# Self-attention band writes: issued by ScalarE on its own DMA queue instead of by the sync engine

## The reference: what is computed

```
scores = q @ k^T                                   # 512 x 512 per head
rel_q[l, r] = q[l] . dist_emb[l - r + 511]         # relative position, query side
rel_k[l, r] = k[r] . dist_emb[l - r + 511]         # relative position, key side
probs = softmax((scores + rel_q + rel_k) / sqrt(32))
ctx   = probs @ v
x1    = layernorm(x + layernorm(ctx @ Wo + bo + x) * gamma + beta)
```

## Time and profile before

| | |
|---|---|
| median of 3 executions | 4623.52 us (4620.94 to 4632.6) |
| profiled execution | 4626.37 us, span 4624.6 us |
| TensorE (PE) busy | 3912.8 us, 85% of the span |
| VectorE (DVE) busy | 2198.7 us, 48% |
| ScalarE (ACT) busy | 1738.2 us, 38% |
| GpSimd (POOL) busy | 1770.0 us, 38% |
| sync engine's DMA queue (q1) | 1158.57 MB, 68.4% of the 16 DMA engines' time |
| ScalarE's DMA queue (q10) | 7.34 MB, 0.4% |

### The profile page before, as it was taken

The page is one execution under the profiler, slowest core; times in us unless marked ns, Lnnn a source line. Parts: engine busy times, 40 slices in busy tenths (PEclk is TensorE's granted clock), DMA queues, the critical chain, the costliest instruction groups (busy, mean ns, idle before and its releaser), DMA issues. The chain is left out here.

```text
span 4624.6 us, 68626 instructions
## 1 busy us (share of the span) xinstructions
PE 3912.8 (85%) x19584; PEld 2380.7 (51%) x19584; DVE 2198.7 (48%) x6132; ACT 1738.2 (38%) x3691; POOL 1770.0 (38%) x1556
## 2 busy tenths in 40 slices
PE   6888888888888886769999999999899566788676
PEld 4666666666666664336666666666544342121144
DVE  4656565656565664854444444444433211111156
ACT  4656565656565663333333333333311110000023
POOL 3656565656565655324444444444411000000012
PEclk9999999999999998989999999999999788888898
DMA  6999898989898996454554445444365326999723
GB/s 265 377 346 363 337 363 335 367 335 373 332 376 331 373 355 252 158 188 155 164 166 153 156 164 167 155 154 164 113 179 166 124 88 274 409 410 411 305 76 134
DMA packets 566768, 1169.16 MB, mean 253 GB/s; under 512 B 35312, under 2 KB 225136, under 8 KB 517360
## 3 DMA queue, kind: packets, MB, share of 16 engines
q1 hardware_dynamic: 561968, 1158.57, 68.4%
q10 hardware_dynamic: 4032, 7.34, 0.4%
q0 software_dynamic: 512, 0.26, 0.0%
HBM read 762.63 MB, written 403.44 MB: 252 GB/s over the span
## 5 line engine op out<-in xcount | busy, mean ns | idle before, releaser
L437 POOL TENSOR_SCALAR a_sc<-a_sc,a_inv 128x512 f32<-128x512 f32 x512 | 809.3, 1582 | 603.4 <-DVE a_inv L387 540.7
L1002 POOL TENSOR_SCALAR b_sc<-b_sc,b_inv 128x128 f32<-128x128 f32 (+3 forms) x512 | 552.7, 1083 | 775.5 <-DVE b_inv L955 775.5
L273 ACT ACTIVATE a_sc<-a_sc,a_mx 128x512 f32<-128x512 f32 x512 | 370.1, 723 | 683.0 <-DVE a_mx L380 682.8
L914 ACT ACTIVATE b_sc<-b_sc,b_mx 128x128 f32<-128x128 f32 (+3 forms) x512 | 287.7, 562 | 815.2 <-DVE b_mx L949 815.1
L960 DVE COPY b_pt<-b_ps_t 128x128 f32<-128x128 f32 (+3 forms) x512 | 248.4, 485 | 575.5 <-PE b_ps_t L862 575.5
L380 DVE CUSTOM_DVE_ANT_0 a_sc<-a_ps_s,a_rq 128x512 f32<-128x512 f32 x512 | 353.3, 690 | 294.8 <-PE a_ps_s L175 263.9
L185 PE MATMUL a_ps_t<-a_ident,a_sc 128*128 128x128 f32 x2048 | 319.7, 279 | 118.6 <-DVE a_pt L394 113.2
L854 PE MATMUL b_ps_s<-b_kT,b_qz 128*128 128x128 f32 (+3 forms) x1024 | 361.0, 434 | 0.8 <-DVE b_mx L949 0.8
L173 PE MATMUL a_ps_s<-a_ks,a_qs 128*128 128x512 f32 x512 | 321.1, 627 | 47.4 <-issue 34.7
L283 ACT ACTIVATE a_stage_q<-a_ps_q 128x640 f32<-128x640 f32 x512 | 350.3, 684 | 18.0 <-PE a_ps_q L198 17.7
L283 ACT ACTIVATE a_stage_k<-a_ps_k 128x640 f32<-128x640 f32 x512 | 354.8, 693 | 1.7 <-DMA band_k<-a_stage_k 1.7
(11 more groups left out here) (202 smaller groups left out, 6264.2 us busy)
## 6 DMA issues: line engine op xcount, KB each, us to landing
band_q<-a_stage_q SPq DMA_DIRECT2D x128, 1280.0 KB, 6.3
band_k<-a_stage_k SPq DMA_DIRECT2D x128, 1280.0 KB, 9.1
a_rk<-band_k SPq DMA_DIRECT2D x128, 1024.0 KB, 11.4
a_rq<-band_q SPq DMA_DIRECT2D x256, 512.0 KB, 11.9
d_w<-in_e_W SPq DMA_DIRECT2D x32, 4096.0 KB, 38.7
b_xT<-x1T SPq DMA_DIRECT2D x64, 1024.0 KB, 5.7
b_cT<-in_ctxT SPq DMA_DIRECT2D x64, 1024.0 KB, 8.3
d_wg<-in_e_Wg SPq DMA_DIRECT2D x16, 4096.0 KB, 28.9
```

Of the source, the lines that this page charges most:

```text
L273: act.activation(sc[n][:, :], sc[n][:, :], ACT.Exp, bias=mx[:, n:n + 1], scale=-1.0, accum_out=sm[:, n:n + 1]).then_inc(sem["a_exped"], 1)
L437: pool.tensor_scalar(sc[n][:, :], sc[n][:, :], inv[:, n:n + 1], None, ALU.mult)\
L914: act.activation(sc[i][:, 0:width(i)], sc[i][:, 0:width(i)], ACT.Exp, bias=mx[:, i:i + 1], scale=-1.0, accum_out=sm[:, i:i + 1]).then_inc( ...
L1002: pool.tensor_scalar(sc[i][:, 0:width(i)], sc[i][:, 0:width(i)], inv[:, i:i + 1], None, ALU.mult).then_inc(sem["b_normed"], 1)
```

## The change

The function `write` and its call leave the sync engine's stream. ScalarE's stream gets a `write` of its own. It is called right behind `stage` when the staged tile was the last of its head, and issues the q and the k write, each behind a wait for the staging copies (its own engine's) and an increment of a new semaphore. Addresses, sizes and completion semaphores of the writes are the same, and so is all that waits for them.

```
# sync engine
-            def write(g, j, h):
-                for kind, st in (("q", stage_q), ("k", stage_k)):
-                    sp.wait_ge(sem[f"a_{kind}_staged"], NT * g + T4 * h + T4)
-                    settle()
-                    out = dr[f"a_band_{kind}"][j % 2, h]
-                    sp.dma_start(out, st[h % 2][:, :, :]).then_inc(sem[f"a_{kind}_written{h % 2}"], 16)
...
                 for h in range(HQ):
-                    if inside(g + 1):
-                        write(g + 1, (j + 1) % 4, h)
                     if h == 0 and inside(g):
                         read(g, j, HQ - 1)
# ScalarE
+            def write(g, j, h):
+                for kind, st in (("q", stage_q), ("k", stage_k)):
+                    act.wait_ge(sem[f"a_{kind}_staged"], NT * g + T4 * h + T4)
+                    act.sem_inc(sem["a_act_waited"], 1)
+                    act.dma_start(dr[f"a_band_{kind}"][j % 2, h], st[h % 2][:, :, :])\
+                       .then_inc(sem[f"a_{kind}_written{h % 2}"], 16)
...
                     if inside(n[0]):
                         stage(*n)
+                        if n[2] % T4 == T4 - 1:
+                            write(n[0], n[1], n[2] // T4)
                     if i == LOAD_AT and j == 2 and inside(g + 2) and not (isinstance(g, int) and g < 0):
                         load_x(g + 2)
```

More of the change, by code:

```diff
@@ L472, in _ @@
             steps(pool, quad)
-A_SEMS = ["a_" + n for n in ["dve_waited", "pool_waited", "sp_waited", "wq_in", "wk_in", "wv_in", "cols_in", "tables_in",
+A_SEMS = ["a_" + n for n in ["dve_waited", "pool_waited", "act_waited", "sp_waited", "wq_in", "wk_in", "wv_in", "cols_in", "tables_in",
                              "ident_in", "hi_stacked", "q_lo", "k_lo", "stacked", "q_staged", "k_staged", "cx_out",
```

## The result

The changed kernel took 4664.21 us (median of 5 executions, 4659.6 to 4667.69), the kernel before 4631.73 us in the same comparison (median of 5 as well). One of those five, 5333.98 us, is an outlier and stays out of the ratio; the other four have a median of 4627.6 us. The ratio is 1.0078, 95% interval 1.0062 to 1.0094: slower by 0.8%, some 36 us. The forecast was 7 us faster, with a range that ended at 4660 us. So the sign was wrong and the time lies just past the range's slow end.

The account below looks back on a forecast made before the run. TensorE with its waits was taken to set the step, with DMA almost full. The terms -12 + 0 + 5 + 0 gave -7 us, to 4617 us, with a range of 4598 to 4660 us.

Parts of the forecast that it names:

- What is removed: Sync engine no longer waits for the next head's staging before issuing reads: -12 us, bounds 0 and -27.
- The 5 us taken for this part: Share of the 9.7 us of steady waits for band reads, 110 to 1740 us, expected to be won.
- The 7 us taken for the two ends: Gain from earlier reads at the self-attention stage's start and end, of at most 17 us.
- What is added on ScalarE: Two write issues for each of 128 heads, expected hidden in slack: 0 us, bounds 0 and +49.
- The block: Time the k write holds ScalarE's queue: 0.54 us, or 0.96 us if the issue takes 0.78.
- The slack of steps 7 and 11: Spare time before TensorE's k bands need the k copies behind the writes: 0.75 and 0.72 us.
- The 0.78 us each for three x loads: Issue cost read for three x loads on ScalarE's queue that meet issues of the sync engine.
- What it is moved past: x loads now stand behind head 3's writes; TensorE waits 0.7 us in 7 places: +5 us, bounds 0 and +15.
- The back edge: Loop edge over quads, TensorE stands 5.49 us on instruction issue: 0 taken, bounds -1 and +1.5 us per edge.
- Rival (b): ScalarE's sequencer held longer by slow issues, costing time from a block of 0.72 us on: 4646 or 4665; chance 0.20.
- (c): Writes land over 13.4 us after issue, ScalarE waits for stage buffers in steps 11 to 15: 4648; chance 0.07.
- (a): Nearly all DMA waits go and x loads stay on time: -14 to -27 us, 4597 to 4610; chance 0.27.

Follow-up runs that it names:

- experiment 10: Changed kernel with x loads and the high part of k ahead of the writes, first seven heads' writes on the sync engine: 0.9992 of the kernel before.
- experiment 11: Experiment 10 with the sync engine's old staging waits put back ahead of its reads: 1.0020 of the kernel before, 13 us slower than experiment 10.
- experiment 6: Experiment 1 with the first seven heads' writes issued by the sync engine in its old order: 1.0029 of the kernel before.
- experiment 7: Experiment 6 with the other writes on ScalarE moved behind the next step's exponential: 1.0000 of the kernel before.
- experiment 9: Experiment 1 with the high part of k made ahead of the head's band writes in step 14: 1.0014 of the kernel before.
- experiment 1: Changed kernel with the four x loads issued ahead of head 3's two band writes on ScalarE: 1.0043 of the kernel before.
- experiment 4: Changed kernel with the sync engine's old staging waits put back, so reads are issued as late as before: 1.0058 of the kernel before.
- experiment 8: Experiment 1 with each k write cut into two DMAs of 640 KB, one more issue per head on ScalarE: 1.0185 of the kernel before.

## Why the prediction was wrong, step by step

**What is removed, -12 us: right for the steady part, wrong for the ends.** The reads are issued earlier, and the steady waits for them, 9.7 us, are gone. The 5 us taken for this part is near the 6 us that the waits of experiment 10 show against the kernel before. The 13 us of experiment 11 agree with the 12 of the prediction by luck, since about half of them makes good what the second queue had taken from the reads. The 7 us taken for the two ends never came. At the start there is a loss, of 6 to 10 us in the time (experiments 6, 7, 10) and 4 to 7 us in the traces up to the first tile. There the DMA engines are the bound: their share is 1.00 at 369 GB/s from 60 to 75 us of the kernel before. One queue served head 0's reads before head 2's writes, which were issued later; with two queues the later writes share the engines with the earlier reads. The two q reads of head 0 landed 11.5 and 11.7 us after issue in the kernel before, 16.1 and 18.2 us in the changed one. The end gained nothing: behind 1740 us the waits for band reads were 15.0 us before and are 15.5 us now, and one of them, for a_rq, is 9.1 us long. That the same sharing is at work there is argued; no experiment was made on it.

**What is added on ScalarE, 0 us: the step that failed.** The block was sized right (0.47 us seen, 0.54 said). The slack of steps 7 and 11 seems to be read right too: experiment 9's trace shows no longer wait behind them. (The 0.78 us each for three x loads was a misreading: that row merges issues of 0.36, 0.36 and 1.31 us and the gaps between them. The sum didn't use it.) What failed is the sentence "Queued behind it are the next exponential, for which VectorE waits, and the next two staging copies". In step 14 the code puts the high part of k behind the write. VectorE's low part waits for it, and then TensorE's v projection, with no slack: its wait was 24.1 us, in 30 pieces of 0.8, before, and is 42.6 us in 29. That is 0.67 us a quad, 21 us in waits, of which 13 us are time (experiment 9). Both facts stood in the kernel and in the list of waits before. The prediction took the consumers from the general order of a step and not from the instruction that follows each of the four places.

**What it is moved past, +5 us: right mechanism, size off.** The x loads cost 16 us (experiment 1). The wait is 3.1 us in each of 7 places against 0.7 taken and 1.1 as upper end: they land 12.4 us after issue, where the prediction had 8.7 plus 1 to 2. It had counted one q read between the writes and the loads. With the reads held (experiment 4) the loads land in 10.2 us, inside that forecast, and TensorE waits 1.8 us in all; so it is the early reads of the other queue, more than one, that were missing. The prediction also left out that ScalarE issues six DMAs in a row there, so that the exponential of step 3 starts 3.72 us after the last copy. By experiment 4 that hold weighs less than the wait. The back edge was right: TensorE waits 34.5 us on issue in 6 places, 34.7 before.

**The sum with measured terms.** The x loads are +16, the high part of k +13, and the start +6 to +10. With all three mended (experiment 10) the kernel stands 4 us under the kernel before, which is not told from zero: 36 - 16 - 13 - 10 is -3. This closes because each edit stands on the one before, so it is no independent check. Experiment 11 splits what is left into +9 with the reads held (ratio 1.0020) and -13 for issuing them early. The +9 is the price of issuing the writes from ScalarE's queue, and no run takes it apart. Its trace lies 4.5 us behind the kernel before in the 24 quads of the steady part and 4.8 us in the last ones, with 15.0 us of steady waits for band reads against 9.7. So reads that share the engines with writes are the likely cause, and late exponentials, whose price experiment 9's trace doesn't show, the less likely one. Each term carries some 5 us of uncertainty.

**The rivals.** Rival (b) named the right engine and a wrong consumer; the k issue stayed at 0.33 us and its point of 0.72 us was not reached. (c) did not come: the k writes land in 11.0 us, under its 13.4, and ScalarE waited 0.4 us for them. Of (a), the steady waits did go, but the x loads did not stay on time. No rival had a loss at a 0.5 us block, so the range ended below the truth.

## What to carry to other kernels

When work is put on an in-order engine, list for every place the very next instructions in that stream, with who waits for each and its slack. Four places with one block need four lists; one in sixteen steps made a third of this loss. Put loads that someone needs soon ahead of large writes on the same queue. A single queue is also an order: with two, a later transfer can take time from an earlier one where DMA is the bound, as at the start here.

## What was not expected of the hardware

A DMA issue on ScalarE costs 0.33 us for each of two writes of 1280 KB in a row, but a third one behind them takes about 1.2 us in the median (experiment 8). The number of issues in a row is not what counts: in experiment 1, where the four x loads of 256 KB come first, six issues in a row take 0.34 to 0.39 us each. Behind the two writes the four x loads took 2.1 to 3.9 us together, against 2.2 to 2.9 us in the kernel before, and 4.9 to 5.0 us in experiment 4. The sync engine shows the same: the issue of a k read behind two writes takes 0.87 us in the median in the kernel before, and 0.36 us in the changed kernel, where no writes stand in its queue. So the price of an issue goes with what its queue already holds, more than with the DMA itself. The reason stays open.
